# v's low part, high part and the ones side by side: one product of 129 columns in place of two, and two sums added on VectorE

## The chip, the core and the metric

The kernel runs on one core of one Trainium2 chip. The metric is the time of one execution on the device in microseconds (us); less is better. The inputs are drawn once and are the same for both kernels.

## The reference

A group norm over 32 groups, q, k and v by 1x1 convolutions, attention of 4 heads with 64 channels each over 1024 pixels, an output convolution and the residual, for 4 images of 256 channels:

```python
x_n = _group_norm(x, gn_w, gn_b)
q = _conv1x1(x_n, wq, bq); k = _conv1x1(x_n, wk, bk); v = _conv1x1(x_n, wv, bv)
q, k, v = (to_heads(q), to_heads(k), to_heads(v))
attn = jnp.einsum('bhqd,bhkd->bhqk', q, k) * scale
attn = jax.nn.softmax(attn, axis=-1)
out = jnp.einsum('bhqk,bhkd->bhqd', attn, v)
out = out.transpose(0, 1, 3, 2).reshape(bsz, c, h, wd)
out = _conv1x1(out, wp, bp)
return x + out
```

All arrays are float32. The kernel reaches that precision with fp16 products: a number is split into a high fp16 part and a low one (the rest), and a product of two numbers is taken as high x high, high x low and low x high, summed in PSUM.

## The kernel before

**Units and slots.** One unit is one head and one half (512 pixels, four query tiles of 128) of one image. There are 8 units in an image and 32 in all; here they are numbered 0 to 31. A unit is worked in four slots, so there are 128 slots. A slot takes two blocks of 128 keys. Each engine has a function `slot(G)` that it runs for G = 0 to 127, so the order on every engine is written out by hand, and semaphores join the engines.

**What PE (TensorE) does in slot G**, in this order: `scores(G)` (L558, products L571 and L572: four products of 512 columns into one of two pairs of banks `st`), the second half of a projection that the slot before began (`job`, L501), a row-maximum product into `mx` (L555), `weigh(G - 4)` (L575, products L594, L596, L597), a second row-maximum product (L555), and the first half of a projection at even G (`job`, bank `gen`). So the first weighing of a unit (slot s = 0) comes on PE behind: one L555, the four score products and another L555, counted from the last weighing of the unit before.

**What weighing is.** `weigh` multiplies the exponentials (`p_hi`, `p_lo`, the stationary operand, 128 x 128) with v (`v_hi`: 64 columns and one column of ones, whose sum is the softmax's denominator; `v_lo`: 64 columns). All four query tiles of a unit have their sums in one PSUM bank, `pv`, 65 columns each. There is only one such bank: the first weighing of the next unit waits for `s_o32` (L583), that is until VectorE has read the bank. In a slot there are 2 key blocks x 4 tiles x 3 = 24 of these products, and each has a weight load of its own.

**What DVE (VectorE) does in slot G**: the low part of v if a v projection has just ended (`low`, L854), the low parts of the exponentials of even slots (`p_low`, L862, two instructions), one row maximum (L843), `normalise` (L865) when a unit's last weighing is over, and a second row maximum. `normalise` waits for the last product of the unit, takes the reciprocals of four denominators (L869), waits with a drain until they are written, and multiplies the four tiles of `pv` with them into `o32` in one instruction (L870), which signals `s_o32`. After a v projection at slot 14 or 30 of an image `low` stands directly behind the slot of a `normalise`; PE's next use of the bank `gen` waits for it (L489).

**The others.** ACT (ScalarE) takes every exponential twice (fp16 `p_hi` and float32), copies projections out of PSUM, and computes the row shift. POOL (GpSimd) takes the low parts of odd slots (L1064) and splits `o32` (L1052, L1054). SP issues the DMAs that duplicate and move q, k and the shift, and the transposes of the output of the attention (L396).

**The end.** In the last image there is no work left to put between: `weigh(124)`, two projections of y, the other weighings, and then the last `normalise`, the transposes on PE (L692), four projections and the sums with x (L891) follow one another.

Memory: `v_hi` has 65 fp16 for each image-half, key block and head, `v_lo` 64. ACT writes `v_hi` (L745) and DVE writes `v_lo` (L854), both through `v_rows` (L311).

Of the kernel before, what the change touches and what calls it, by code (L numbers as in the profile page):

```python
# [12 lines left out]
def attention_block(nc, x, gn_w, gn_b, wq, bq, wk, bk, wv, bv, wp, bp, out):  # L13
# [63 lines left out]
    with ctx:  # L77
# [48 lines left out]
        v_hi = sb("v_hi", [P, CT, NK, 2, PV], F16)  # L126
        v_lo = sb("v_lo", [P, CT, NK, 2, D], F16)
# [29 lines left out]
        pv_v = pv[:, 0:QT * PV].rearrange("p (t n) -> p t n", n=PV)  # L157
# [153 lines left out]
        def v_rows(tile, i, j):  # L311
            return tile[:, i, 4 * j:4 * j + 4, :, 0:D].rearrange("p c h d -> p (c h) d")
# [164 lines left out]
        def _(pe):  # L477
# [66 lines left out]
            def statistic(kind, b):  # L544

                wait(pe, *((s_mv, b + 1) if kind == "mean" else (s_dev, b + 1)))
                nc.tensor.matmul(pv[:, QT * PV:QT * PV + CT], group_avg[:, :], mv[:, :, 0] if kind == "mean" else dev2[:, :],
                                 start=False, stop=True, skip_group_check=True).then_inc(s_stat, 1)
                taken.append((s_gmean if kind == "mean" else s_gvar, b + 1))
# [25 lines left out]
            def weigh(G):  # L575
# [10 lines left out]
                for c in range(CPS):  # L586
# [3 lines left out]
                    vh, vl = v_hi[:, head // 2, k, head % 2, :], v_lo[:, head // 2, k, head % 2, :]  # L590
                    for q in range(QT):
                        qs = slice(q * P, (q + 1) * P)
                        hi, lo = p_hi[:, G % PR, c, qs], p_lo[:, G % PR, c, qs]
                        nc.tensor.matmul(pv_v[:, q, :], hi, vh, start=k == 0 and q == 0,  # L594
                                         stop=False, skip_group_check=True)
                        nc.tensor.matmul(pv_v[:, q, 0:D], hi, vl, start=False, stop=False, skip_group_check=True)  # L596
                        last = nc.tensor.matmul(pv_v[:, q, :], lo, vh, start=False,  # L597
                                                stop=k == NK - 1, skip_group_check=True)
# [236 lines left out]
        def _(dve):  # L835
            def then(ins):

                dve.drain()
# [26 lines left out]
            def normalise(U):  # L865
# [3 lines left out]
                then(nc.vector.reciprocal(rden[:, U % 2, :], pv_v[:, :, D]))  # L869
                nc.vector.tensor_tensor(o32[:, half, :, (U % 2) * D:(U % 2 + 1) * D], pv_v[:, :, 0:D],  # L870
                                        rden[:, U % 2, :].unsqueeze(2).to_broadcast([P, QT, D]), ALU.mult)\
                  .then_inc(s_o32, 1)
# [57 lines left out]
            def statistic(kind, b):  # L930

                result = pv[:, QT * PV:QT * PV + CT]
# [24 lines left out]
            nc.vector.memset(v_hi[:, :, :, :, D], QKV_SCALE / O_SCALE).then_inc(s_ones, 1)  # L957
# [186 lines left out]
```

## Time and profile before

| | |
|---|---|
| median of 3 runs | 386.52 us (384.23 to 386.55) |
| the profiled execution | 385.64 us |
| its span, first to last instruction | 383.9 us |
| PE busy | 361.5 us (94% of the span) |
| ACT busy | 310.7 us (81%) |
| DVE busy | 307.8 us (80%) |
| POOL busy | 259.8 us (68%) |
| granted TensorE clock | 1.0 of full speed in all 40 slices |

The page's matmuls overlap in their rows: a product of 65 columns has a row of 194 ns, while the next one starts 30 ns later. What a product costs a full PE is read from the starts of its neighbours in the timeline, not from its mean.

From the timeline, at each of the 31 places where one unit's weighing ends and the next one's begins: the time from the end of L870 (`o32` is ready) to the start of the first L594 of the next unit.

| from L870's end to the next unit's first product, ns | after units | how many |
|---|---|---|
| 56 to 57 | 0, 1, 2, 27, 28, 29, 30 | 7 |
| 69 | 11 (L870 itself began 0.36 us late) | 1 |
| 175, 193 | 15, 7 | 2 |
| 424 to 430 | 4, 8, 9, 10, 16, 17, 18, 19, 22, 23, 24, 25, 26 | 13 |
| 444, 447, 465 | 6, 14, 20 | 3 |
| 569, 698, 770, 993, 1010 | 13, 5, 12, 3, 21 | 5 |

### The profile page before, as it was taken

What the parts mean: (1) busy time and instruction counts of PE and PEld (TensorE: products, weight loads), DVE (VectorE), ACT (ScalarE), POOL (GpSimd) and SP (SyncE); (2) the same over time, 40 slices, a digit from 0 to 9 for tenths busy, and PEclk for the clock granted to TensorE, in tenths of its full rate; (3) what the DMA queues carried; (4) which work ended last, traced back from release to release, by engine and by line L of the source; (5) the groups of instructions that cost most, each with busy time, mean ns of one, the idle gap of its engine ahead of it and who ended that gap; (6) DMA issues with size and microseconds to landing.
All of it is one profiled execution on the core that took longest, in us unless ns stands there. A gap on an engine that the chain in (4) does not pass through costs nothing.

```text
span 383.9 us, 11261 instructions
## 1 busy us (share of the span) xinstructions
PE 361.5 (94%) x4593; PEld 227.7 (59%) x4593; DVE 307.8 (80%) x565; ACT 310.7 (81%) x392; POOL 259.8 (68%) x226
## 2 busy tenths in 40 slices
PE   2898799999999999999999999999999999999876
PEld 1644455656666566755666666665756566665554
DVE  4869987889878788889888788888878888899543
ACT  1847789988787999988787999988878888898940
POOL 5045559768577896949668796958765784759820
PEclk9999999999999999999999999999999999999999
DMA  6055401241633430241633430121633430151012
GB/s 219 8 118 171 104 4 43 29 138 31 138 111 70 105 78 28 76 133 30 144 119 71 97 84 30 35 64 35 139 120 71 103 81 27 29 167 29 3 40 99
DMA packets 38731, 30.92 MB, mean 81 GB/s; under 512 B 23820, under 2 KB 31512, under 8 KB 38680
## 3 DMA queue, kind: packets, MB, share of 16 engines
q1 hardware_dynamic: 38656, 30.20, 31.2%
q8 instruction: 36, 0.59, 0.7%
q14 instruction: 15, 0.12, 0.1%
q10 hardware_dynamic: 24, 0.01, 0.0%
HBM read 9.44 MB, written 4.19 MB: 36 GB/s over the span
## 4 chain that ended last, share of the span: by engine, by line
PE 66%; SPq 8%; ACT 6%; POOL 5%; issue 5%; DVE 4%; DMA 4%; POOLq 1%; DVEq 0%; ACTq 0%
PE gen L501 14%; PE st L571 10%; PE st L572 10%; PE mx L555 9%; PE pv L594 6%; PE pv L597 6%; PE pv L596 6%; POOL p_lo L1064 3%; SPq L396 3%; PE st L501 3%; DMA q_max<-shift 2%; ACT p_hi L769 2%; DVE mx L843 1%; SPq L375 1%; DMA xin<-in_x_dram 1%
## 5 line engine op out<-in xcount | busy, mean ns | idle before, releaser
L843 DVE TENSOR_REDUCE mx<-mx 128x1 f32<-128x512 f32 x256 | 173.1, 686 | 32.8 <-PE mx L555 25.7
L769 ACT ACTIVATE p_hi<-st 128x1024 f16<-128x1024 f32 x128 | 131.4, 1027 | 41.8 <-PE st L572 40.9
L1064 POOL TENSOR_TENSOR p_lo<-p,p_hi 128x1024 f16<-128x1024 f32 x63 | 134.3, 2132 | 23.8 <-ACT p L774 23.6
L594 PE MATMUL pv<-v_hi,p_hi 128*128 128x65 f16 x1024 | 105.8, 194 | 1.6 <-DVE o L870 1.5
L597 PE MATMUL pv<-v_hi,p_lo 128*128 128x65 f16 x1024 | 106.0, 194 | 0.0
L596 PE MATMUL pv<-v_lo,p_hi 128*128 128x64 f16 x1024 | 105.8, 193 | 0.0
L571 PE MATMUL st<-q_twice,k_both 128*128 128x512 f16 x256 | 97.2, 380 | 6.4 <-DMA q_max<-shift 4.2
L594 PEld LDWEIGHTS pv<-v_hi,p_hi 128*128 128x128 f16 x1024 | 94.5, 98 | 14.4 <-DVE o L870 4.4
L596 PEld LDWEIGHTS pv<-v_lo,p_hi 128*128 128x128 f16 x1024 | 93.6, 98 | 14.0
L862 DVE TENSOR_TENSOR p_lo<-st,p_hi 128x512 f16<-128x512 f32 x130 | 83.6, 684 | 21.8 <-ACT st L774 20.3
L572 PE MATMUL st<-q_max,k_one 65*128 65x512 f16 x256 | 97.3, 380 | 0.0
L555 PE MATMUL mx<-k_both,q_twice 128*128 128x512 f16 x244 | 92.3, 381 | 1.7 <-DMA k_one<-st_hi_k 1.2
L597 PEld LDWEIGHTS pv<-v_hi,p_lo 128*128 128x128 f16 x1024 | 93.7, 97 | 0.0
L774 ACT ACTIVATE st<-st 128x1024 f32<-128x1024 f32 x65 | 66.5, 1023 | 0.0
L774 ACT ACTIVATE p<-st 128x1024 f32<-128x1024 f32 x63 | 64.4, 1023 | 0.0
L571 PEld LDWEIGHTS st<-q_twice,k_both 128*128 128x128 f16 x256 | 25.3, 99 | 31.5 <-DMA q_max<-shift 7.1
L572 PEld LDWEIGHTS st<-q_max,k_one 65*128 65x128 f16 x256 | 25.1, 98 | 25.6
L555 PEld LDWEIGHTS mx<-k_both,q_twice 128*128 128x128 f16 x244 | 27.7, 114 | 18.0 <-DVE mx L843 3.0
L347 POOL TENSOR_TENSOR st_lo_k<-e_k,st_hi_k 128x512 f16<-128x512 f32 x16 | 18.5, 1156 | 10.5 <-ACT e_k L742 8.5
L1038 POOL CAST st_hi_k<-e_k 128x512 f16<-128x512 f32 x14 | 8.6, 611 | 24.2 <-ACT e_k L742 15.9
L501 PE MATMUL gen<-w_hi_v,z_hi 128*128 128x128 f16 x128 | 23.0, 219 | 0.3 <-DVE v_lo L854 0.2
L501 PE MATMUL gen<-w_hi_v,z_lo 128*128 128x128 f16 x128 | 23.0, 219 | 0.0
(171 smaller groups left out, 473.9 us busy)
## 6 DMA issues: line engine op xcount, KB each, us to landing
q_twice<-st_hi_q SPq DMA_DIRECT2D x64, 64.0 KB, 2.1
xres<-in_x_dram SPq DMA_DIRECT2D x4, 1024.0 KB, 5.2
out_dram<-y SPq DMA_DIRECT2D x14, 256.0 KB, 2.5
xin<-in_x_dram SPq DMA_DIRECT2D x6, 512.0 KB, 4.5
k_both<-st_hi_k SPq DMA_DIRECT2D x16, 128.0 KB, 2.3
k_one<-st_hi_k SPq DMA_DIRECT2D x16, 128.0 KB, 2.3
k_both<-st_lo_k SPq DMA_DIRECT2D x16, 128.0 KB, 2.3
q_max<-st_lo_q SPq DMA_DIRECT2D x32, 64.0 KB, 2.2
```

The lines of the kernel that those rows point to most:

```text
L501: last = nc.tensor.matmul(dst, a, c, start=first and t == 0 and n == 0, stop=t == CT - 1 and n == 2, skip_group_check=True)
L555: nc.tensor.matmul(mxb[j % 2][:, :], q_twice[:, head, tile_of(half, tile)], k_both[:, head, halves(part)], start=True, stop=True).then_inc ...
L571: nc.tensor.matmul(dst, k_both[:, head, k], q_twice[:, head, q], start=True, stop=False)
L572: last = nc.tensor.matmul(dst, k_one[:, head, k], q_max[:, head, q], start=False, stop=True)
L594: nc.tensor.matmul(pv_v[:, q, :], hi, vh, start=k == 0 and q == 0, stop=False, skip_group_check=True)
L596: nc.tensor.matmul(pv_v[:, q, 0:D], hi, vl, start=False, stop=False, skip_group_check=True)
L597: last = nc.tensor.matmul(pv_v[:, q, :], lo, vh, start=False, stop=k == NK - 1, skip_group_check=True)
L769: nc.scalar.activation(p_hi[:, G % PR, :, :], scores, ACT.Exp, scale=SM_SCALE / M_SCALE)
L774: nc.scalar.activation(p_full(G), scores, ACT.Exp, scale=SM_SCALE / M_SCALE).then_inc(s_exp, 1)
L843: nc.vector.reduce_max(mx8[:, U % 2, tile, part:part + 1], mxb[j % 2][:, :], AX.X)\
L862: nc.vector.tensor_tensor(p_lo[:, G % PR, c, :], p_full(G)[:, c, :], p_hi[:, G % PR, c, :], ALU.subtract).then_inc(s_plo_dve, 1)
L1064: nc.gpsimd.tensor_tensor(p_lo[:, G % PR, :, :], p_full(G), p_hi[:, G % PR, :, :], ALU.subtract)\
```

## The change

v's three parts are laid side by side in one array `v_all`: 64 columns low, 64 columns high, one of ones. Of the four query tiles of a unit, tile 0 keeps its three products. For tiles 1 to 3 the two products with `p_hi` as stationary operand (65 columns of `v_hi` and 64 of `v_lo`, which fell on the same 64 sums) become one product of 129 columns, which puts the sum with the low part into 64 columns of its own. The product with `p_lo` and `v_hi` stays. The bank `pv` now holds 65 + 3 x 129 = 452 columns, and the two statistics that share the bank move behind them. VectorE adds the two sums: `normalise` multiplies the main sums of tiles 0 to 2 in one instruction and those of tile 3 in another, drains, and then takes for each of tiles 1 to 3 one more instruction (low sum x reciprocal + `o32`). The signal `s_o32` comes from the last of them.

```diff
-        v_hi = sb("v_hi", [P, CT, NK, 2, PV], F16)
-        v_lo = sb("v_lo", [P, CT, NK, 2, D], F16)
+        v_all = sb("v_all", [P, CT, NK, 2, 2 * D + 2], F16)
+        v_lo, v_hi = v_all[:, :, :, :, 0:D], v_all[:, :, :, :, D:2 * D]
...
+        STEP = 2 * D + 1
+        STAT = (QT - 1) * STEP + PV
+        pv_sum = [pv[:, q * STEP:q * STEP + PV] for q in range(QT)]
+        pv_low = [pv[:, q * STEP - D:q * STEP] for q in range(QT)]
...
                     for q in range(QT):
                         qs = slice(q * P, (q + 1) * P)
                         hi, lo = p_hi[:, G % PR, c, qs], p_lo[:, G % PR, c, qs]
-                        nc.tensor.matmul(pv_v[:, q, :], hi, vh, start=k == 0 and q == 0,
-                                         stop=False, skip_group_check=True)
-                        nc.tensor.matmul(pv_v[:, q, 0:D], hi, vl, start=False, stop=False, skip_group_check=True)
-                        last = nc.tensor.matmul(pv_v[:, q, :], lo, vh, start=False,
-                                                stop=k == NK - 1, skip_group_check=True)
+                        if q == 0:
+                            nc.tensor.matmul(pv_sum[q], hi, vh, start=k == 0, stop=False, skip_group_check=True)
+                            nc.tensor.matmul(pv_sum[q][:, 0:D], hi, v[:, 0:D], start=False, stop=False,
+                                             skip_group_check=True)
+                        else:
+                            nc.tensor.matmul(pv[:, q * STEP - D:q * STEP + PV], hi, v[:, 0:STEP], start=False,
+                                             stop=False, skip_group_check=True)
+                        last = nc.tensor.matmul(pv_sum[q], lo, vh, start=False, stop=k == NK - 1,
+                                                skip_group_check=True)
...
-                then(nc.vector.reciprocal(rden[:, U % 2, :], pv_v[:, :, D]))
-                nc.vector.tensor_tensor(o32[:, half, :, (U % 2) * D:(U % 2 + 1) * D], pv_v[:, :, 0:D],
-                                        rden[:, U % 2, :].unsqueeze(2).to_broadcast([P, QT, D]), ALU.mult)\
-                  .then_inc(s_o32, 1)
+                cols = slice((U % 2) * D, (U % 2 + 1) * D)
+                then(nc.vector.reciprocal(rden[:, U % 2, :], pv[:, D:STAT:STEP]))
+                most = pv[:, 0:(QT - 1) * STEP].rearrange("p (t n) -> p t n", n=STEP)[:, :, 0:D]
+                nc.vector.tensor_tensor(o32[:, half, 0:QT - 1, cols], most,
+                                        rden[:, U % 2, 0:QT - 1].unsqueeze(2).to_broadcast([P, QT - 1, D]), ALU.mult)
+                then(nc.vector.tensor_scalar(o32[:, half, QT - 1, cols], pv_sum[QT - 1][:, 0:D],
+                                             rden[:, U % 2, QT - 1:QT], None, ALU.mult))
+                for q in range(1, QT):
+                    last = nc.vector.scalar_tensor_tensor(out=o32[:, half, q, cols], in0=pv_low[q],
+                                                          scalar=rden[:, U % 2, q:q + 1], in1=o32[:, half, q, cols],
+                                                          op0=ALU.mult, op1=ALU.add)
+                last.then_inc(s_o32, 1)
```

On DVE, at the end of any unit, these rows stood in the kernel before (L843 the row maxima, L869 and L870 `normalise`):

```order
L843 TENSOR_REDUCE mx<-mx 128x1
L869 RECIPROCAL rden<-pv 128x4
L870 TENSOR_TENSOR o<-pv,rden 128x4x64
```

and in the changed one these stand there (the row maxima are L851 now, `normalise` is L878 to L885):

```order
L851 TENSOR_REDUCE mx<-mx 128x1
L878 RECIPROCAL rden<-pv 128x4
L880 TENSOR_TENSOR o<-pv,rden 128x3x64
L882 TENSOR_SCALAR o<-pv,rden 128x64
L885 SCALAR_TENSOR_TENSOR o<-pv,rden,o 128x64 x3
L851 TENSOR_REDUCE mx<-mx 128x1 x3
```

Two instructions became six, at the same place between two row maxima. On PE, the end of one unit's weighing, and what comes before the next unit's first product, before:

```order
L594 MATMUL pv<-v_hi,p_hi 128x65
L596 MATMUL pv<-v_lo,p_hi 128x64
L597 MATMUL pv<-v_hi,p_lo 128x65
L555 MATMUL mx<-k_both,q_twice 128x512
L571 MATMUL st<-q_twice,k_both 128x512
L572 MATMUL st<-q_max,k_one 128x512
L571 MATMUL st<-q_twice,k_both 128x512
L572 MATMUL st<-q_max,k_one 128x512
L555 MATMUL mx<-k_both,q_twice 128x512
L594 MATMUL pv<-v_hi,p_hi 128x65
```

and in the changed kernel:

```order
L603 MATMUL pv<-v_all,p_hi 128x129
L605 MATMUL pv<-v_all,p_lo 128x65
L558 MATMUL mx<-k_both,q_twice 128x512
L574 MATMUL st<-q_twice,k_both 128x512
L575 MATMUL st<-q_max,k_one 128x512
L574 MATMUL st<-q_twice,k_both 128x512
L575 MATMUL st<-q_max,k_one 128x512
L558 MATMUL mx<-k_both,q_twice 128x512
L599 MATMUL pv<-v_all,p_hi 128x65
L600 MATMUL pv<-v_all,p_hi 128x64
```

The six products between two units are the same; only the weighing's own products have changed. In one slot there are 2 x (3 + 3 x 2) = 18 of these in place of 24.

## Rows read from the trace of the kernel before

**Rows 1.** The page's first part: busy time (share of the span) and instructions.

```profile
PE 361.5 (94%) x4593; PEld 227.7 (59%) x4593; DVE 307.8 (80%) x565; ACT 310.7 (81%) x392; POOL 259.8 (68%) x226
```

**Rows 2.** Busy time by stretch, us from the start: length, PE, PEld, DVE, ACT, POOL.

```profile
70.00:342.00 272.00, 269.58 (x3527) 171.49 (x3526) 228.46 (x404) 236.13 (x293) 199.56 (x167) 1.00 0.34 84
```

**Rows 3.** Timeline: start us, duration us, engine, line; end of unit 16.

```profile
226.43 0.19 PE L597 MATMUL pv<-v_hi,p_lo 128*128 128x65 f16 x1
...
226.46 0.38 PE L555 MATMUL mx<-k_both,q_twice 128*128 128x512 f16 x1
...
226.66 0.18 DVE L869 RECIPROCAL rden<-pv 128x4 f32<-128x4 f32 x1
...
226.92 0.42 DVE L870 TENSOR_TENSOR o<-pv,rden 128x256 f32<-128x256 f32 x1
...
227.26 0.68 DVE L843 TENSOR_REDUCE mx<-mx 128x1 f32<-128x512 f32 x1
...
227.77 0.19 PE L594 MATMUL pv<-v_hi,p_hi 128*128 128x65 f16 x1
```

**Rows 4.** Timeline: one weighing of 24 products, then 12 products of 128 columns.

```profile
200.71 0.19 PE L594 MATMUL pv<-v_hi,p_hi 128*128 128x65 f16 x1
...
201.43 0.38 PE L555 MATMUL mx<-k_both,q_twice 128*128 128x512 f16 x1
...
201.65 0.22 PE L501 MATMUL gen<-w_hi_v,z_hi 128*128 128x128 f16 x1
...
202.32 0.38 PE L571 MATMUL st<-q_twice,k_both 128*128 128x512 f16 x1
```

**Rows 5.** Groups by line and form: xcount, busy us, mean ns; idle before.

```profile
L870 DVE TENSOR_TENSOR o<-pv,rden 128x256 f32<-128x256 f32 x32 | 13.6, 425 | 2.7 <-issue 0.4
...
L849 DVE TENSOR_REDUCE mx<-mx 128x4 f32<-128x8 f32 x32 | 5.2, 161 | 1.1
...
L891 DVE SCALAR_TENSOR_TENSOR y<-st,xres 128x256 f32<-128x256 f32 x4 | 1.7, 425 | 1.5 <-PE st L501 1.5
...
L891 DVE SCALAR_TENSOR_TENSOR y<-mx,xres 128x512 f32<-128x512 f32 x1 | 0.7, 680 | 0.0
...
L936 DVE TENSOR_SCALAR veps<-pv 128x2 f32<-128x2 f32 x2 | 0.3, 148 | 0.0
```

**Rows 6.** Timeline: VectorE and PE at the end of unit 14 (v projection).

```profile
205.46 0.42 DVE L870 TENSOR_TENSOR o<-pv,rden 128x256 f32<-128x256 f32 x1
...
206.33 0.19 PE L594 MATMUL pv<-v_hi,p_hi 128*128 128x65 f16 x1
...
206.46 0.68 DVE L854 SCALAR_TENSOR_TENSOR v_lo<-gen,v_hi 128x512 f16<-128x512 f32 x1
...
207.28 0.38 PE L501 MATMUL gen<-z_hi,w_hi_k 128*128 128x512 f16 x1
```

**Rows 7.** The chain that ended last, in order of time: around unit 2.

```profile
72.90 0.42 DVE o L870
73.33 0.60 DVE mx L843
73.92 0.61 DVE v_lo L854
74.53 0.14 issue
74.67 0.38 PE gen L501
```

**Rows 8.** The same chain, units 27, 30 and 31.

```profile
344.12 0.44 DVE o L870
344.55 0.05 issue
344.60 0.20 PE pv L594
...
369.73 0.44 DVE o L870
...
376.18 0.44 DVE o L870
```

**Rows 9.** The same chain at a transpose and key copies on SP's queue.

```profile
266.60 0.51 SPq L385
...
278.90 2.10 DMA q_max<-shift
```

More of the change, by code:

```diff
@@ L156, in attention_block @@
         tail_banks = [st[0][:, 0:512], st[0][:, 512:1024], st[1][:, 0:512], st[1][:, 512:1024]]
-        pv_v = pv[:, 0:QT * PV].rearrange("p (t n) -> p t n", n=PV)
+        STEP = 2 * D + 1
+        STAT = (QT - 1) * STEP + PV
+        pv_sum = [pv[:, q * STEP:q * STEP + PV] for q in range(QT)]
+        pv_low = [pv[:, q * STEP - D:q * STEP] for q in range(QT)]
         s_w = {n: sem(f"s_w_{n}") for n in "kqvp"}
@@ L311, in v_rows @@
         def v_rows(tile, i, j):
-            return tile[:, i, 4 * j:4 * j + 4, :, 0:D].rearrange("p c h d -> p (c h) d")
+            return tile[:, i, 4 * j:4 * j + 4, :, :].rearrange("p c h d -> p (c h) d")
         def p_full(G):
@@ L546, in statistic @@
                 wait(pe, *((s_mv, b + 1) if kind == "mean" else (s_dev, b + 1)))
-                nc.tensor.matmul(pv[:, QT * PV:QT * PV + CT], group_avg[:, :], mv[:, :, 0] if kind == "mean" else dev2[:, :],
+                nc.tensor.matmul(pv[:, STAT:STAT + CT], group_avg[:, :], mv[:, :, 0] if kind == "mean" else dev2[:, :],
                                  start=False, stop=True, skip_group_check=True).then_inc(s_stat, 1)
@@ L589, in weigh @@
                     k = CPS * s + c
-                    vh, vl = v_hi[:, head // 2, k, head % 2, :], v_lo[:, head // 2, k, head % 2, :]
+                    v = v_all[:, head // 2, k, head % 2, :]
+                    vh = v[:, D:STEP]
                     for q in range(QT):
@@ L930, in statistic @@
             def statistic(kind, b):
-                result = pv[:, QT * PV:QT * PV + CT]
+                result = pv[:, STAT:STAT + CT]
                 if kind == "mean":
@@ L955, in first_z_low @@
                                             ALU.subtract).then_inc(s_z0_lo, 1)
-            nc.vector.memset(v_hi[:, :, :, :, D], QKV_SCALE / O_SCALE).then_inc(s_ones, 1)
+            nc.vector.memset(v_all[:, :, :, :, 2 * D], QKV_SCALE / O_SCALE).then_inc(s_ones, 1)
             for t in range(CT):
```

## The prediction, made before the changed kernel was run

> **What bounds the kernel now.** I read the page's busy shares first. PE is busy for 94% of the span, and ACT and DVE for about 80% each [rows 1]. The stretches say more than the mean: from 70 to 342 us PE is busy for 269.6 of 272 us [rows 2]. There PE is the bound, and a stall put on it lengthens the run by its own size, while DVE has some 44 us of idle time in the same stretch. Time goes away only if PE's work shrinks, and comes in wherever PE has to wait for something new. Before 70 us and after 342 us ACT, DVE and POOL take turns with PE.
>
> Then I looked for the place where DVE's work touches PE: the hand-over of the one `pv` bank between two units. At the end of unit 16 the last product of the unit starts at 226.43 and the reciprocal starts at 226.66. L870 ends at 227.34, and the next unit's first product starts at 227.77, directly after its predecessors on PE [rows 3]. Between the two weighings PE has six long products and no wait, 1.34 us from start to start. Where PE does wait for L870, the distance from its end (344.55) to the product (344.60) is 0.05 to 0.06 us [rows 8]. So the slack of the hand-over is 0.43 - 0.06 = 0.37 us in this place. The table of the 31 hand-overs gives the slack of each in the same way: distance less 0.057 us.
>
> **PE: what is saved.** A weighing has 24 products and takes 201.43 - 200.71 = 0.72 us, 30 ns for each [rows 4]. The 12 products of 128 columns behind it take 202.32 - 201.65 = 0.67 us, 55.8 ns each [rows 4]. One product of 129 columns is then 56.2 ns. Two products with their loads (60 ns) become one of 56.2: 3.8 ns saved. The timeline's starts are rounded to 10 ns, so 0.72 us may be 0.71, 29.6 ns for a product, and the saving then 3.0 ns. I take 3.2 ns, times 6 in a slot = 19 ns. A load and a product have gone, but the columns have not: 194 for each tile before and after. Over the 24 units from 3 to 26 (96 slots) this is 1.8 us; elsewhere PE is not the bound and I count nothing. Ends of the term: 1.4 (at 2.5 ns) and 2.2 us (at 3.8 ns).
>
> The Trainium skill, TensorE: Matmul & The Clock Gate, section "Back-to-back issue gap", has a rule by which this change would be worth far more: in a stream of weight loads and products both set the spacing, about 81 ns for products of 128 columns. By that, a load costs some 25 ns beside its product, and 768 loads less would be about 19 us (an estimate from that page). This trace does not agree: the same products stand 55.8 ns apart with a load before each.
>
> **DVE: what is added to the hand-over.** Start-to-start distances first. L870 (256 elements) to the next instruction is 227.26 - 226.92 = 0.34 us, though its row is 0.425 [rows 3, 5]: the next one starts 0.085 us before it ends. The slope is from L891: 680 ns for 512 elements and 425 for 256, so 1.0 ns per element [rows 5], and a pitch is 1.0 x n + 75 to 85 ns, a duration 1.04 x n + 160 ns. Small instructions lie on that line or under it (161 for 8 elements, 148 for two from PSUM) [rows 5].
> - Reciprocal start to the first multiply, drain included: 0.26 us, as now.
> - TENSOR_TENSOR of 3 x 64: pitch 0.265 us.
> - TENSOR_SCALAR of 64 and a drain: duration about 0.216, and then the 0.075 us that stand between the end of L869 and the start of L870 (226.84 to 226.92) [rows 3]: 0.29 us.
> - Two SCALAR_TENSOR_TENSOR of 64 at a pitch of 0.131 us, and a third to its end, 0.216 us: 0.48 us.
> The sum is 1.29 us from the reciprocal's start to `s_o32`; before it was 0.68 [rows 3]. The signal comes **0.61 us later**, and DVE is free 0.61 us later too.
>
> Bounds of that 0.61: the lower one has TENSOR_SCALAR and the three adds each at the fixed cost alone (148 ns, pitch 78), +0.37 us. The upper one has no overlap at all, each instruction beginning where the last ends: 0.26 + 0.36 + 0.23 + 0.075 + 3 x 0.226 = 1.60, so +0.92. I stay at 0.61, since the pitch of L870 itself shows the overlap and L891 shows this very instruction at this slope.
>
> The upper bound is what the Trainium skill, VectorE: DVE Perf Modes, section "The DRAIN you can't avoid", would have: the next instruction does not start until the pipe is empty. The trace does not agree, since the row maximum behind L870 starts 0.08 us before L870 ends.
>
> **Where it lands.** The stall at a hand-over is 0.61 less its slack.
> - 14 hand-overs with a slack of 0.37 (the 13 of 424 to 430 ns, and unit 11, whose late start I take for chance): 0.24 each. Three with 0.39, 0.39 and 0.41: 0.64 together. Unit 13 (0.51): 0.10. Units 7 and 15 (0.14 and 0.12): 0.96. Units 3, 5, 12, 21: nothing. Sum 5.06 us.
> - Two of these (units 4 and 20) lie inside stretches in which the chain runs through SP's queue anyway, as from 266.6 to 278.9 [rows 9]; PE waits there later for copied keys or the shift. I take 0.44 off: **4.6 us**.
> - After units 6, 10, 14, 18, 22 the low part of v follows on DVE. At unit 14 it ends at 207.14 and the product that needs `gen` starts 0.14 us later, at 207.28, at once after the wait [rows 6]; there is no slack (0 to 0.04 us in the five). PE is held for 0.61 or 0.58 there, not 0.22 to 0.24. That adds **1.8 us**.
> - On the chain itself: unit 2, where L870, a row maximum, the low part of v and `gen` follow one another [rows 7]; unit 27, unit 30 and unit 31 [rows 8]. 4 x 0.61 = **2.4 us**. Units 0, 1, 28, 29 wait for L870 too, but the chain passes by ACT and POOL there; I count nothing.
>
> Nothing else moves: the row maximum behind `normalise` is 0.61 us later, and so is the product that waits for its bank, but PE is late as well and keeps more than 0.1 us of slack; POOL reads `o32` two slots later. The copies into `v_all` write as many elements as before.
>
> Sum: 4.6 + 1.8 + 2.4 - 1.8 = +7.0 us. Against the profiled execution's own 385.64 that is 392.7. The median of the three runs is 0.9 above it; I predict the middle of the two sums, **393.1 us**. Each 10 ns of the added chain is worth about 0.25 us, as some 25 places pay it.
>
> **The rivals.**
> - *The chain is shorter than I think* (not slower). Several small instructions run close to the fixed cost. The decisive point is +0.47 us instead of +0.61: below it the sum is under 3.9 us, within 1%. At +0.45 it is 385.6 + 3.3 = 389 us. Even at +0.37, where the 14 ordinary hand-overs pay nothing, the rest costs 1.3 us net. For it: the small rows [rows 5]. Against: 64 elements must pass, and L891's slope holds. 17%.
> - *The instructions do not overlap* (+0.92, or a pointer operand that costs more): 385.6 + 14.5 = 400 us. For it: the adds read what the instructions before them wrote. Against: the row maximum starts early behind L870 [rows 3], and the drain is already in my sum. 8%.
> - *Weight loads set the pitch*, not columns (faster): a pair costs 30 ns whatever its width, 768 x 30 = 23 us saved, 385.6 - 23 + 8.8 = 371 us. Against: 55.8 ns for 128 columns at the same load [rows 4]. 2%.
> - *DVE becomes late for good*: maxima and low parts of the exponentials fall behind and stall PE a second time, say 0.15 us at 20 hand-overs, 396 us. Against: 44 us of idle DVE in the long stretch [rows 2]. 10%.
>
> **How the numbers follow.** My forecast has 63%, and its own range is 390.5 to 395.5. The range that takes in half of the short chain and the second stall is 389.5 to 397. A measurement of this kernel can tell about 1% from no change (3.9 us). Slower by over 1%: forecast, no overlap, lasting lateness: 81%. Within 1%: the short chain, 17%. Faster by over 1%: 2%.
>
> **What the profile would show.** PE: groups L603 and L605 with 768 and 1024 products, and a weighing of 0.70 us in place of 0.72. DVE: from the reciprocal to the end of the third add 1.29 us, and the distance from there to the next unit's first product 0.06 us at about 25 hand-overs; the waits "PEld pv <- DVE o" grow from ten to some 25. After units 6, 10, 14, 18, 22 PE waits for `v_lo` by 0.3 to 0.4 us. I am wrong if the chain takes under 1.1 us, if PE's stalls are taken back later in the unit, or if weighing falls well under 0.69 us.

## The result, and the profile of the changed kernel

The changed kernel takes **403.17 us** (median of 4 runs, 402.24 to 405.78) against 386.53 us before (4 runs): a ratio of **1.044, interval 1.040 to 1.049**. It is slower by 4.4%, more than the 1.7% of the forecast and outside its range. The profiled execution took 402.24 us with a span of 400.5 us; that of before had 385.64 and 383.9. So there are 16.6 us to account for. (One execution of `job_first`, further down, took 950 us for a reason that stays open, and its time there is the median of the other three.)

The first part of the page, which answers to [rows 1]:

```profile
PE 364.2 (91%) x3825; PEld 224.0 (56%) x3825; DVE 329.8 (82%) x693; ACT 311.1 (78%) x392; POOL 260.0 (65%) x226
```

768 pairs of load and product are gone, and DVE has 128 instructions and 22 us of work more. The long stretch, which answers to [rows 2], and the four microseconds from 42 to 46 us (length, then PE, PEld, DVE, ACT, POOL, then the granted clock as a share of full speed, DMA share, GB/s):

```profile
42.00:46.00 4.00, 4.00 (x29) 2.39 (x27) 3.30 (x6) 2.05 (x3) 2.53 (x2) 0.59 0.61 133
...
70.00:342.00 272.00, 262.23 (x2813) 161.75 (x2810) 234.94 (x485) 227.43 (x283) 194.06 (x164) 1.00 0.31 77
```

PE now idles 9.8 us of this stretch, where it idled 2.4. This is where the idle time comes from, by the list of waits (who, in which line, for what: us in total, times, longest):

```profile
PEld pv L599 <- DVE o L885: 25.9, 27, 1.8
...
PE pv L599 <- DVE o L885: 13.8, 27, 1.6
```

The same wait in the kernel before:

```profile
PE pv L594 <- DVE o L870: 1.5, 5, 0.8
```

It stalled PE at 5 hand-overs, and now 27 of the 31 stall it. The loads' waits overlap with products still running, so I read PE's own 13.8 us. The chain that ended last, at the end of unit 16, shows one of them (start us, us, what), answering to [rows 3]:

```profile
233.74 0.02 issue
233.76 0.18 DVE rden L878
233.95 0.03 DVEq L846
233.98 0.04 issue
234.02 0.36 DVE o L880
234.38 0.19 DVEq L846
234.57 0.07 issue
234.65 0.68 DVE o L885 x3
235.32 0.05 issue
235.37 0.20 PE pv L599
```

From the reciprocal to the end of the third add 1.56 us pass, where 0.68 passed before; the next unit's first product stands 0.05 us behind it. The median over the hand-overs is 1.55 us. The groups of DVE's instructions (count, then busy us, mean ns) say where the length is:

```profile
L885 DVE SCALAR_TENSOR_TENSOR o<-pv,rden,o 128x64 f32<-128x64 f32 x96 | 21.3, 278 | 2.4
L880 DVE TENSOR_TENSOR o<-pv,rden 128x192 f32<-128x192 f32 x32 | 11.4, 358 | 2.7 <-issue 0.4
...
L882 DVE TENSOR_SCALAR o<-pv,rden 128x64 f32<-128x64 f32 x32 | 8.8, 275 | 0.0
```

The three-tile product takes the 0.36 us that the prediction gave it. L885 and L882 take 0.278 and 0.275 where it had 0.216.

**Where the 16.6 us lie.** For every unit I took the start of the first product of its first weighing in both traces. The starts of units 7 and 27 before, then after:

```profile
118.85 0.19 PE L594 MATMUL pv<-v_hi,p_hi 128*128 128x65 f16 x1
...
335.86 0.19 PE L594 MATMUL pv<-v_hi,p_hi 128*128 128x65 f16 x1
```

```profile
121.32 0.20 PE L599 MATMUL pv<-v_all,p_hi 128*128 128x65 f16 x1 [0.38 <-DVE veps L952]
...
348.02 0.20 PE L599 MATMUL pv<-v_all,p_hi 128*128 128x65 f16 x1 [0.33 <-DVE o L885]
```

The lead of before grows from 2.5 to 12.2 us in these twenty units, and to 16.6 at the end of the span. The same measurement for the main experiments (their labels are explained below), in us against the profiled execution of before:

| kernel | chain | up to unit 1 | units 1 to 7 | units 7 to 27 | unit 27 to end |
|---|---|---|---|---|---|
| changed | 1.55 | +2.50 | -0.04 | +9.70 | +4.47 |
| `dve_alone` | 1.55 | +1.56 | +0.35 | +10.85 | +4.67 |
| `no_pointer` | 1.30 | +0.78 | -0.86 | +5.10 | +7.38 |
| `one_add` | 1.17 | +0.37 | -1.41 | +3.14 | +6.40 |
| `no_add` | 0.81 | +0.69 | -1.29 | -0.34 | +0.27 |
| `pe_alone` | 0.68 | +1.56 | -1.70 | -1.27 | -0.24 |
| `reduce_behind` | 0.68 | +2.24 | +1.37 | +9.16 | +2.37 |

"Chain" is the time from the reciprocal's start to the end of the instruction that signals.

The column "units 1 to 7" shows that lateness is taken back there. In the kernel before, PE waits in these units for copies made by DMA, and a PE that comes later finds them landed. These are two of its waits between 42 and 110 us:

```profile
PE mx L555 <- DMA k_one<-st_hi_k: 0.7, 1, 0.7
PE st L571 <- DMA q_max<-shift: 0.4, 1, 0.4
```

In the changed kernel the first of them is gone in this stretch and the second is 0.3 us. Together with PE's saving this makes up for the hand-overs of units 1 to 6, which do stall PE.

### The profile page after: what moved, and what is told of

Read it like the earlier page. It is cut to its first block, busy times and chain, and to the rows that moved or that the text cites. A ratio compares the mean times of both kernels' runs of the same rounds, so it can differ in the third digit from the quotient of the medians.

```text
span 400.5 us, 9885 instructions
## 1 busy us (share of the span) xinstructions
PE 364.2 (91%) x3825; PEld 224.0 (56%) x3825; DVE 329.8 (82%) x693; ACT 311.1 (78%) x392; POOL 260.0 (65%) x226
## 4 chain that ended last, share of the span: by engine, by line
PE 52%; DVE 13%; issue 11%; POOL 11%; ACT 7%; POOLq 2%; DVEq 2%; DMA 1%; SPq 0%; ACTq 0%
PE gen L504 14%; PE pv L603 7%; PE st L575 7%; PE st L574 7%; PE mx L558 6%; POOL p_lo L1080 6%; PE pv L605 5%; DVE o L885 4%; DVE mx L851 3%; PE st L504 2%; ACT p_hi L777 2%; ACT p L782 2%; DVE o L880 2%; PE pv L599 2%; DVEq L846 2%
## 5 line engine op out<-in xcount | busy, mean ns | idle before, releaser
L851 DVE TENSOR_REDUCE mx<-mx 128x1 f32<-128x512 f32 x256 | 171.7, 685 | 30.3 <-PE mx L558 24.6
L1080 POOL TENSOR_TENSOR p_lo<-p,p_hi 128x1024 f16<-128x1024 f32 x63 | 134.3, 2132 | 32.3 <-ACT p L782 32.3
L605 PE MATMUL pv<-v_all,p_lo 128*128 128x65 f16 x1024 | 103.4, 193 | 0.0
L870 DVE TENSOR_TENSOR p_lo<-st,p_hi 128x512 f16<-128x512 f32 x130 | 83.3, 682 | 16.6 <-ACT st L782 16.5
L603 PE MATMUL pv<-v_all,p_hi 128*128 128x129 f16 x768 | 95.6, 220 | 0.0
L605 PEld LDWEIGHTS pv<-v_all,p_lo 128*128 128x128 f16 x1024 | 85.0, 97 | 0.0
L603 PEld LDWEIGHTS pv<-v_all,p_hi 128*128 128x128 f16 x768 | 69.7, 97 | 0.0
L599 PE MATMUL pv<-v_all,p_hi 128*128 128x65 f16 x256 | 49.7, 194 | 15.0 <-DVE o L885 13.8
L600 PE MATMUL pv<-v_all,p_hi 128*128 128x64 f16 x256 | 49.2, 192 | 0.0
L599 PEld LDWEIGHTS pv<-v_all,p_hi 128*128 128x128 f16 x256 | 24.9, 97 | 37.1 <-DVE o L885 25.9
L600 PEld LDWEIGHTS pv<-v_all,p_hi 128*128 128x128 f16 x256 | 24.9, 97 | 11.6 <-issue 0.3
L1054 POOL CAST st_hi_k<-e_k 128x512 f16<-128x512 f32 x14 | 8.6, 611 | 24.9 <-ACT e_k L750 16.6
```

The costliest lines, as they stand in the source:

```text
L599: nc.tensor.matmul(pv_sum[q], hi, vh, start=k == 0, stop=False, skip_group_check=True)
L600: nc.tensor.matmul(pv_sum[q][:, 0:D], hi, v[:, 0:D], start=False, stop=False, skip_group_check=True)
L603: nc.tensor.matmul(pv[:, q * STEP - D:q * STEP + PV], hi, v[:, 0:STEP], start=False, stop=False, skip_group_check=True)
L605: last = nc.tensor.matmul(pv_sum[q], lo, vh, start=False, stop=k == NK - 1, skip_group_check=True)
L851: nc.vector.reduce_max(mx8[:, U % 2, tile, part:part + 1], mxb[j % 2][:, :], AX.X)\
L870: nc.vector.tensor_tensor(p_lo[:, G % PR, c, :], p_full(G)[:, c, :], p_hi[:, G % PR, c, :], ALU.subtract).then_inc(s_plo_dve, 1)
```

## The experiments

**PE's side alone, and DVE's side alone.** `pe_alone` is the changed kernel with DVE's two instructions of before. It reads columns 0, 128, 256 and 384 of the bank and adds no low sums, so its output is not the attention's:

```diff
...
+                nc.vector.tensor_tensor(o32[:, half, :, (U % 2) * D:(U % 2 + 1) * D],
+                                        pv[:, 0:QT * 2 * D].rearrange("p (t n) -> p t n", n=2 * D)[:, :, 0:D],
+                                        rden[:, U % 2, :].unsqueeze(2).to_broadcast([P, QT, D]), ALU.mult)
```

> The changed kernel's products and layout, with VectorE's old two instructions at the end of a unit: one multiply of four tiles from columns 0, 128, 256, 384 of the bank, so its numbers are not the attention's. If the hand-over of the bank costs the time (theory), this kernel keeps only TensorE's saving: a weighing of 0.70 us in place of 0.72, about -1.8 us against the kernel before, so 384 to 385 us. If the 129-column products or the new layout cost the time (rival), it stays near the changed kernel, above 398 us. If a saved weight load were worth more than 3 ns, it would fall below 380 us.

Measured: 383.85 us, ratio 0.995 (0.992 to 0.998). In units 7 to 27 it gains 1.27 us. The products of 129 columns stand 55 to 57 ns from the next start, those of 65 columns 29 to 30, so the columns set the pitch, and a load taken away gave no more than the few ns of the prediction. What the change was good for on PE is real and small, as the prediction sized it.

`dve_alone` is the kernel before with the six DVE instructions on its old bank (the three adds follow as in the change, and read `pv_v`):

```diff
+                nc.vector.tensor_tensor(o32[:, half, 0:QT - 1, cols], pv_v[:, 0:QT - 1, 0:D],
+                                        rden[:, U % 2, 0:QT - 1].unsqueeze(2).to_broadcast([P, QT - 1, D]), ALU.mult)
+                then(nc.vector.tensor_scalar(o32[:, half, QT - 1, cols], pv_v[:, QT - 1, 0:D],
+                                             rden[:, U % 2, QT - 1:QT], None, ALU.mult))
...
```

> The kernel before with VectorE's six instructions in the place of two; the adds read the main sums in place of low ones, so the output is wrong. Theory (late signal, 1.55 us from the reciprocal to it in place of 0.68, so 0.87 late against a slack of 0.37): 31 hand-overs with 0.5 us or more each, +16 to +19 us, so 403 to 405 us, some 2 us above the changed kernel. Rival (products or layout): near 386.5 us. If both share the loss it lies between, near 394.

Measured: 403.11 us, ratio 1.045 (1.039 to 1.051), the same loss as the whole change. The whole times hide a difference of the clock (last section): all four executions of `dve_alone` had a mean granted clock of 1.000, and none of the changed kernel's. Units 7 to 27 are free of that: there `dve_alone` loses 10.85 us and the changed kernel 9.70, and the 1.15 between them is PE's saving (1.27 in `pe_alone`). So the loss is DVE's, and the layout and PE's products have no part in it.

**Why the chain is 0.26 us longer than predicted.** `no_pointer` is the changed kernel with a constant where TENSOR_SCALAR and the three adds read the reciprocal:

```diff
-                                             rden[:, U % 2, QT - 1:QT], None, ALU.mult))
+                                             0.001, None, ALU.mult))
...
-                                                          scalar=rden[:, U % 2, q:q + 1], in1=o32[:, half, q, cols],
+                                                          scalar=0.001, in1=o32[:, half, q, cols],
```

> The changed kernel with constants in the place of the pointer scalars of the tile-3 multiply and the three adds (so tiles 1 to 3 are wrong). The adds stood 0.20 us apart, not 0.13 as I had it, and had 278 ns, not 216. If the pointer scalar is the price (theory), they go back to 0.13 apart and the chain from the reciprocal to the signal to 1.29 us, as in the sum: +7 us or so against before, 394 to 396 us. If it is the add's form or the PSUM source (rival), the chain stays at 1.55 us and the time near 403 us.

Measured: 397.98 us, ratio 1.030 (1.024 to 1.037), and in the groups of its DVE instructions:

```profile
L885 DVE SCALAR_TENSOR_TENSOR o<-pv,o 128x64 f32<-128x64 f32 x96 | 15.5, 217 | 2.4
...
L882 DVE TENSOR_SCALAR o<-pv 128x64 f32<-128x64 f32 x32 | 6.9, 214 | 0.0
```

These are the 0.216 us of the prediction. The pitch of the adds is 131 and 141 ns in place of 192 and 200, and the chain 1.30 us in place of 1.55, where the prediction had 1.29. Three of the four executions had a lowered clock near the end (last section) and took 397.95 us or more; the one without it took 395.26, inside the 394 to 396 that was expected. So **a scalar operand that is read per partition costs each of these instructions 60 ns**, in its duration and in the distance to the next one. Four of them stand on the chain: 0.24 of the missing 0.26 us. The same in another form can be read on ScalarE (groups of the changed kernel; the row without a bias tile, then with one, both 512 elements out of a bank):

```profile
L753 ACT ACTIVATE v_all<-gen 128x512 f16<-128x512 f32 x16 | 9.7, 609 | 1.4 <-PE gen L504 1.4
...
L750 ACT ACTIVATE e_q<-gen,bias_s_q 128x512 f32<-128x512 f32 x13 | 9.0, 695 | 0.0
```

The difference is 86 ns. These two rows also differ in the type of the result. With f16 results in both, out of `st`, the groups of L821 (no bias tile, 597 ns, one instruction) and L747 (a bias tile, 688 ns, two instructions) differ by 91 ns. The Trainium skill, ScalarE: Activation LUTs, section "What ACT_TABLE_LOAD costs", gives about 93 ns for each such operand on ScalarE; the rows agree within 10 ns.

**How the chain's length turns into time.** `no_add` leaves out the second drain and the three adds, so all low sums are missing from its output; `one_add` keeps the drain and the add of tile 1. The edit of `one_add`:

```diff
-                for q in range(1, QT):
+                for q in range(1, 2):
```

> The changed kernel without the second drain and the three adds (the low sums are left out). The chain from the reciprocal to the signal is 0.26 + 0.275 + 0.275 = 0.81 us, 0.13 later than in the kernel before and inside the usual slack of 0.37. Threshold theory: only the places without slack pay (8 units by 0.13, the low parts of v 5 by some 0.11): +1.1 to +1.6 us on the 383.9 us of the kernel with the products alone, 385 to 385.5 us. Rival (every hand-over pays in proportion, 19.3 us for 0.87): +2.9, 386.8 us.

> The changed kernel with the add of tile 1 alone (tiles 2 and 3 without their low sums). The chain is 1.16 us, 0.48 later than before. Threshold theory: 0.11 at 14 hand-overs, 0.3 at two, up to 0.48 at the low parts of v and at 4 to 8 units without slack: +6.2 to +8.1 us on 383.9, so 390 to 392 us. Rival (in proportion): +10.6, 394.5 us.

Measured: `no_add` 384.73 us, ratio 0.993 (0.990 to 0.996), chain 0.81; `one_add` 394.05 us, ratio 1.017 (1.014 to 1.021), chain 1.17. With `no_pointer` and the changed kernel that makes four lengths of one chain. I put each measured chain into the slacks on which the prediction was built (a stall of the added length less the slack at ordinary hand-overs, the whole added length where the low part of v follows). From this I took off 1.27 us for PE, which is not the prediction's term but what `pe_alone` measured. For units 7 to 27 this gives -0.86, +2.49, +5.03 and +9.50 us; measured are -0.34, +3.14, +5.10 and +9.70. The model of the hand-over holds for the four lengths in these twenty units, with a miss of at most 0.65 us. The rival, a loss in proportion to the added length, would give +0.3, +4.9 and +6.6 us for the first three (an estimate, scaled from the changed kernel's 9.70 with PE's 1.27 set apart). It is too high by 0.7, 1.7 and 1.5 us. By whole times one would have read `one_add` the other way: the slack theory had 390 to 392 us, the rival 394.5, and 394.05 was measured. The table shows where that comes from, since 6.40 of its 8.5 us lie behind unit 27, most of them under a lowered clock (last section). So the model was good, and the length it was fed was wrong.

**Is it only the hand-over, or DVE's time too?** Two kernels leave the signal of before where it is and put work behind it. `reduce_behind` adds to the kernel before one row maximum of 780 elements:

```diff
+                nc.vector.reduce_max(spare[:, :], rest[:, :], AX.X)
```

> Again the kernel before with 0.87 us more VectorE work behind the signal in each unit, now one maximum over 780 elements of one spare SBUF array, which reads a single SBUF tensor. Theory (late signal; the 481 us of the try with multiply-adds came from their two SBUF inputs beside GpSimd, whose rows had 1.2 to 2.1 us each): the hand-overs keep their time, the five low parts of v come up to 0.85 later and unit 2 0.87: +3 to +5 us, 390 to 391.5 us. Rival (occupancy of VectorE): 402 us or more.

Measured: 400.26 us, ratio 1.034 (1.031 to 1.037). The theory of the late signal (390 to 391.5 us) failed here, and the rival of DVE's occupancy (402 or more) came within 2 us. The list of its waits says which engine waits now:

```profile
PEld mx L557 <- DVE mx L845: 12.1, 31, 0.7
PE mx L557 <- DVE mx L845: 6.7, 22, 0.6
```

PE's second row-maximum product after a weighing needs the bank that the row maximum behind `normalise` empties. In the kernel before, that row maximum starts at 227.26 [rows 3] and so ends at 227.94; the product starts at 228.50:

```profile
228.50 0.39 PE L555 MATMUL mx<-k_both,q_twice 128*128 128x512 f16 x1
```

That is a slack of 0.56 - 0.06 = 0.50 us, and at the ordinary hand-overs it is the same within 0.05. DVE comes free 0.87 us later, which is 0.37 us short there. With each hand-over's own slack, and the whole 0.87 where the low part of v follows, I get 9.5 us for units 7 to 27 (an estimate); measured are 9.16. In the changed kernel this wait does not grow, since PE is held by the same DVE work ahead of it. This is its row, 2.7 us, and that of before has 3.0 us:

```profile
PEld mx L558 <- DVE mx L851: 2.7, 8, 0.5
```

So the two prices are not added. The hand-over's is the larger and comes first on PE, 0.87 - 0.37 = 0.50 us at an ordinary unit; 0.37 of that would be paid to this second wait even if the bank were free on time. It means that 0.87 us of DVE work for each unit costs some 13 us even when the bank is handed over on time. The prediction's "PE is late as well and keeps more than 0.1 us of slack" was right for the change and would have misled about any version that only moves the signal forward.

`work_behind` adds behind the signal what the change adds, on spare arrays: a drain, four instructions of 64 elements with a pointer, a drain.

```diff
+                dve.drain()
+                for q in range(QT):
+                    nc.vector.scalar_tensor_tensor(out=spare[:, q, :], in0=rest[:, q, :],
+                                                   scalar=rden[:, U % 2, q:q + 1], in1=rest[:, q, :],
+                                                   op0=ALU.mult, op1=ALU.add)
+                dve.drain()
```

> The kernel before with the same amount of VectorE work more at the end of each unit (four multiply-adds of 64 elements with a pointer scalar and two drains, some 0.9 us), but on spare SBUF arrays and behind the signal that frees the bank. Theory (only the lateness of the signal costs): the hand-overs are untouched; what stays is the low part of v behind it, 5 times up to 0.85 us = 4 us, and up to 0.9 us at unit 2; so 389 to 391 us. Rival (VectorE's occupancy, wherever it lies): like the changed kernel's loss, 402 us or more.

Measured: 481.1 us, ratio 1.250 (1.240 to 1.259). This kernel did not answer its question, because it measures something else. Its clock was lowered too (a mean of 0.936 and less), so not all of the loss is the instructions' own. Its instructions by line (duration ns min/median/max) and, in the timeline, one set of four on DVE and what GpSimd does then:

```profile
L877 DVE SCALAR_TENSOR_TENSOR spare<-rest,rden x124: 270/283/2132, 65.1 to 470.6; 128x64 f32<-128x64 f32 x124
```

```profile
354.30 2.42 DVE L877 SCALAR_TENSOR_TENSOR spare<-rest,rden 128x64 f32<-128x64 f32 x4
```

```profile
353.93 2.12 POOL L1073 TENSOR_TENSOR p_lo<-p,p_hi 128x1024 f16<-128x1024 f32 x1 [0.81 <-ACT p L776]
```

Both inputs of L877 are in SBUF, and an instruction of 0.28 us takes up to 2.13 us. Of the 128, 51 take over 0.4 us, and each of these ends 76 to 87 ns after a GpSimd instruction ends; here that is 353.93 + 2.12 = 356.05, and the first of the four ends at 356.14. The adds of the change read one input from PSUM and one from SBUF, and none of the 96 took over 285 ns, beside the same GpSimd work. The Trainium skill, SBUF — State Buffer, section "Who interferes with whom", states this: a VectorE instruction with two SBUF inputs contends with a GpSimd instruction that reads SBUF, through a port pair that is locked exclusively. The trace agrees, with the 51 of 128. By these rows, copying the sums to SBUF and adding them there on DVE would be worse than the change; no run tried it.

**Can the idea be saved?** `copy_out` lets DVE only copy the bank out in units 0 to 29, which frees it, and gives the additions and the multiplication to GpSimd a slot later:

```diff
+                if U < B * UNITS - 2:
+                    wait(dve, s_o32, U - 1)
+                    nc.vector.tensor_copy(pvs[:, U % 2, 0:STAT], pv[:, 0:STAT]).then_inc(s_copied, 1)
+                    return
...
+                then(nc.gpsimd.tensor_tensor(most, most, tiles[:, 0:QT - 1, D + 1:STEP], ALU.add))
+                nc.gpsimd.tensor_tensor(o32[:, half, :, (U % 2) * D:(U % 2 + 1) * D], tiles[:, :, 0:D],
+                                        rden[:, U % 2, :].unsqueeze(2).to_broadcast([P, QT, D]), ALU.mult)
```

> A version meant to keep the saving. For units 0 to 29 VectorE only copies the 452 columns of the bank to SBUF (some 0.63 us, less than the 0.68 of reciprocal and multiply) and signals the bank free; the denominators' reciprocals follow one slot later, and GpSimd adds the low sums and multiplies. The last two units go as in the changed kernel. Theory: the hand-over is as early as in the kernel before, so TensorE's saving of 1.8 to 2.5 us stays, less 2 x 0.87 at the end, if GpSimd (68% busy, some 1.1 us more per unit, 77%) keeps up: 384.5 to 386.5 us. Rival (GpSimd falls behind in the slots with its split of the output, and low parts of the exponentials come late): 390 us or more.

Measured: 392.99 us, ratio 1.015 (1.012 to 1.018). In the steady part it works: 452 columns are copied in 0.63 us, and at unit 30 it is 0.77 us ahead of the kernel before. All of the loss comes behind that, 7.35 us behind at the end. Its chain there:

```profile
365.64 0.61 POOL o_hi L1092
366.30 1.19 POOLq L77
367.49 2.09 POOL p_lo L1104
369.62 0.61 PE st L577
```

Four GpSimd instructions for the unit before stand ahead of the last low part of an exponential, on which PE's scores wait; and when PE starts again, its clock is at half speed:

```profile
369.00:380.00 11.00, 8.71 (x77) 5.75 (x78) 3.29 (x9) 1.94 (x2) 0.57 (x1) 0.53 0.05 10
```

`job_first` and `job_first_2` (the same edit; the trace read here is that of the second) keep the six instructions, but in the first slot of a unit put a half projection ahead of the weighing on PE, which gives DVE 0.65 us more:

```diff
+                todo = job_at(G)
+                early = todo and G % SPU == 0 and G >= 20 and place(G)[1] not in (0, 16)
+                if early:
+                    job(*todo, only=0)
```

> The changed kernel, with one thing moved on TensorE: in the slot that begins a unit (not at slots 0 and 16 of an image, where the projection waits for v's low part) the half projection stands ahead of the unit's first weighing instead of behind it. That gives the hand-over 0.65 us more work as cover: slack 1.02 in place of 0.37 us, against 0.87 of lateness. Slack theory: the ordinary hand-overs pay nothing; the v hand-overs keep their 0.85 us. From unit 7 to unit 27, where the changed kernel lost 9.7 us, this one loses 2 us; the whole is 7 to 8 us below the changed kernel, 394 to 396 us. Rival (VectorE's added work itself, or the products, cost the time): within 2 us of the changed kernel, 401 us or more.

> The kernel job_first once more, for a trace of an undisturbed execution. By the slack theory the gap between two units' weighings is 1.99 us at the ordinary hand-overs and nothing is waited for (the first product 0.2 us after the third add, not 0.06), while the five v hand-overs keep a gap of 1.83 us and wait; from unit 7 to 27 the loss is 2 to 4 us in place of 9.7. The y projection at slot 4 of an image waits 0.65 us for ScalarE's copy, as in mixed.

Measured: `job_first` 393.64 us with a ratio of 1.020 (1.016 to 1.025); `job_first_2` 395.72 us, one execution. In units 7 to 27 the loss falls from 9.70 to 3.30 us, where 2 had been expected. What stays is where no work is there to be put ahead, where the low part of v follows on DVE, and twice 0.40 us where the work put ahead waits for its own bank. Order buys back two thirds of the loss in these units. This run does not tell the hand-over from the second wait that `reduce_behind` showed, since the product of the row maximum comes 0.65 us later too. The list of waits does: in the changed kernel PE waits 27 times for the bank, 13.8 us in all, and for the row maximum no more than before.

`mixed` takes the wide products only in units 3 to 25 without those behind which a low part of v comes (18 units; the expectation counted 17), with the work put ahead as in `job_first`, and the old form elsewhere. `mixed_2` leaves out units 7, 15 and 23 as well (15 units are left), and does not put the work ahead in the image's slot 4.

```diff
+        def wide(U):
+            return 3 <= U < 26 and U % 4 != 2
```

> The version that the ledger points to: the wide products and the six instructions only in 17 units from 3 to 25 whose hand-over has the projection ahead of the weighing; all other units (0 to 2, each fourth, where v's low part follows, and 26 to 31) keep the three products and the two instructions of the kernel before. Slack theory: no new stall, and 17 x 4 x 19 ns = 1.3 us saved: 0.3% under the kernel before, 385.3 us at a median of 386.6. Rival (a projection half that is moved ahead costs something later in the unit, or the maximum behind the six instructions is late): 387 us or more.

> mixed without its one new stall: there the y projection at slot 4 of an image, moved ahead, waited 0.65 us for ScalarE to empty its bank, twice between unit 7 and unit 27. Here that slot keeps its old order and the units before it (7, 15, 23) the old products, so 14 units are wide. Slack theory: no stall of more than 0.05 us that the kernel before doesn't have, 14 x 4 x 19 ns = 1.1 us saved, 385.5 us at a before of 386.6, a ratio of 0.997. Rival: at or above the kernel before again.

Measured: `mixed` 387.56 us, ratio 1.003 (1.001 to 1.006); `mixed_2` 387.10, ratio 1.003 (1.001 to 1.006). In `mixed` every one of the added chains is hidden, but at units 7 and 15 the work put ahead comes too early for its own bank (timeline, with the wait in brackets):

```profile
130.48 0.71 ACT L766 ACTIVATE e_q<-gen,bias_s_q 128x512 f32<-128x512 f32 x1
...
131.25 0.39 PE L509 MATMUL gen<-oT_hi,w_hi_p 128*128 128x512 f16 x1 [0.49 <-ACT e_q L766]
```

`mixed_2` takes that away and is 0.36 us faster than before in units 7 to 27. It is 1.3 us behind at unit 1, 0.15 at unit 7 and 1.4 at the end. The last part comes behind unit 27, where PE waits 0.98 and 1.25 us for copies of the shift; neither `mixed` nor the kernel before has waits of that size there, and why is open. No version that computes everything beat the kernel before: the gain to be had is 19 ns for each of 60 slots, about 1 us, too little to show against what the start and the end cost.

## Why the prediction was wrong

1. **What bounds the kernel**: right. PE is the bound in the long stretch, and the hand-over of the `pv` bank is where DVE touches it. `dve_alone` has the whole loss.
2. **PE's saving of 1.8 us**: right within its ends. `pe_alone` gained 1.27 us over the 20 units from 7 to 27, which is 1.5 over the 24 counted. The pitch of the wide product is 56 ns, as worked out. The rival in which the loads set the pitch (371 us) is refuted by the 383.85 us of `pe_alone`. The about 81 ns for a product of 128 columns behind a weight load, which the Trainium skill, TensorE: Matmul & The Clock Gate, section "Back-to-back issue gap", has, do not fit these runs either: here it is 56 ns.
3. **The added chain of 0.61 us**: this is the step that failed. It measured **0.87 us**. Part by part, as predicted and as measured: reciprocal to multiply 0.26 and 0.26; three tiles 0.265 and 0.275; TENSOR_SCALAR with drain 0.29 and 0.35; the adds 0.131, 0.131 and 0.216 against 0.200, 0.192 and 0.278. "L891 shows this very instruction at this slope" was the false sentence. L891 has a constant for its scalar [rows 5], the adds read theirs from `rden`, and this costs 60 ns four times. The measured value lies inside the bounds of 0.37 and 0.92, but my range of the time did not reach as far as the upper bound: that case had 8% as a rival, "a pointer operand that costs more: 400 us", and was cut off with the range at 397. Rows that could have warned me were in the profile of before too, among ScalarE's groups: 512 elements with and without a bias tile, 688 and 597 ns. I looked at the DVE rows alone.
4. **Instructions overlap**: right. The row maximum starts before the last add ends, and with constants the adds stand 0.13 to 0.14 us apart. The prediction set this against the Trainium skill, VectorE: DVE Perf Modes, section "The DRAIN you can't avoid"; that section also says that a next op that is not held starts earlier, and with that the rows agree.
5. **Slack of the hand-overs, and the whole length where the low part of v follows**: right in units 7 to 27, over four chain lengths. With 0.87 us the prediction's own 0.25 us for each 10 ns adds 6.5 us to its 7.0, so 399.1 us for an execution that took 402.24.
6. **"Units 0, 1, 28, 29: I count nothing"**: wrong for three of the four. Behind unit 27 the loss is 4.47 us; units 27, 30 and 31 make 3 x 0.87 = 2.6, and units 28 and 29 pay about 0.8 each, 1.6 together. The chain there does go through ACT and POOL, but what they wait for has itself become later. Unit 0 pays too: in `dve_alone`, whose clock stayed up, the lateness grows from 0.68 to 1.56 us from the first product of unit 0 to that of unit 1. Against that, units 1 and 2 pay nothing on balance, where the prediction had 0.61 for unit 2: from unit 1 to unit 3 the lateness changes by -0.15 us in the changed kernel and by -0.04 in `dve_alone`.
7. **"A stall put on it lengthens the run by its own size"**: this holds from unit 7 on, and not before it. Up to unit 1 the changed kernel is 2.50 us late, of which 0.87 is the hand-over of unit 0 and about 1.6 came with the fallen clock of the next section. To unit 7 it does not get later, largely because PE's waits for DMA copies shrink. `pe_alone`, with the same fall of the clock, is 1.56 us late at unit 1 and 0.14 early at unit 7. So how much of the clock's share reaches the end of the changed kernel is not shown.
8. **The rest**, about 1.5 us of the 16.6, has no single place. I set the prediction's sum, with 0.87 us in it, against the table: the changed kernel is about 0.65 us later at unit 7 than the sum has it, loses about 0.6 more in units 7 to 27, and 0.25 more behind them than point 6 counts (estimates).
9. **"DVE late for good"** did not happen: outside the hand-overs the waits for DVE did not grow (the row-maximum wait went from 3.0 to 2.7 us).

The direction was right. The mistake was of size, and it was taken from a row whose instruction had the same name but another kind of operand.

## What to carry to other kernels

Price a small instruction by a row with the same name, the same source (PSUM or SBUF) and the same kind of scalar operand; if there is none, the range has to reach to the dear bound. Before work is taken off the engine that bounds a kernel and put on another at the place where it hands over a buffer, compare the gain for each round (here 4 x 19 = 76 ns) with what the added chain has beyond the slack (0.87 - 0.37 = 0.50 us). And look at the second waiter too: an engine's time behind its signal has a slack of its own, 0.50 us here, and moving the signal forward does not help once that is used up.

## What the runs showed of the hardware that I had not expected

- **A scalar read per partition costs a VectorE instruction 60 ns** beside the same instruction with a constant (278 and 217 ns for 64 elements, SCALAR_TENSOR_TENSOR; 275 and 214, TENSOR_SCALAR), and the next one starts 60 ns later. On ScalarE a bias tile costs 86 to 91 ns.
- **A VectorE instruction with two SBUF inputs was blocked for up to 1.85 us** while GpSimd worked on SBUF (270 to 2132 ns); with one input in PSUM none of 96 was (273 to 285 ns), though 74 of them ran beside a GpSimd instruction.
- **The clock fell to its lower level near 42 us in some executions.** The rows of the same stretch, for `no_add` and for `pe_alone`, whose products on PE are the same:

```profile
42.00:46.00 4.00, 4.00 (x51) 2.78 (x50) 3.72 (x7) 2.91 (x4) 3.11 (x2) 1.00 0.59 130
```

```profile
42.00:46.00 4.00, 4.00 (x29) 2.65 (x27) 2.83 (x6) 1.94 (x2) 2.46 (x2) 0.60 0.61 132
```

  In 4 us PE executes 29 products in place of 51. Ahead of it PE had been idle for 2.2 us in either case, waiting for the shift's transfer. From 42.7 to 46.1 us the changed kernel had the 1.2 GHz level and then 2.4 GHz again. It was so in the profiled executions of `pe_alone`, `reduce_behind`, `work_behind`, `copy_out`, `job_first_2`, `mixed` and `mixed_2` too, and not in those of the kernel before, `dve_alone`, `no_add`, `no_pointer` and `one_add`; so it goes with no part of the change. The kernel before has both kinds of execution as well: of its 57 beside the experiments, 32 had a mean granted clock of 0.996 or 0.995, and the median of these was 1.1 to 2.6 us above that of the other 25 on each of four chips. What decides it stays open.
- **After a late stall the clock fell in some kernels.** In `copy_out`, `one_add` and `no_pointer` it was at the lower level for 10.2 us, from 369.2, 371.3 and 374.7 us on (mean granted clock 0.983 to 0.987), in or just behind an idle time of PE of 4.1, 1.7 and 1.8 us. In the changed kernel and in `dve_alone` PE idled for 1.9 us at the same work (until 382.3 and 383.0 us) and the clock stayed up, so the stall alone does not decide it. Behind unit 27 `no_pointer` and `one_add` lose 7.38 and 6.40 us; the changed kernel's 4.47, scaled by the added chain, would give 3.2 and 2.5, so about 4 us go with the clock (an estimate). The changed kernel's own slower executions belong here too: 402.24 and 402.33 us at a mean clock of 0.996 and 0.995, 404.02 at 0.992 and 405.78 at 0.987. The row of `no_pointer`:

```profile
374.50:381.00 6.50, 5.10 (x42) 3.41 (x43) 3.22 (x10) 1.94 (x2) 0.00 (x0) 0.51 0.01 3
```
